# A two-layer decoder kernel: the first attention's bias inside its output product and its weight splits on ScalarE and VectorE, a third buffer for heads, and paired value products in the grouped attentions

## The chip, the cores and the metric

The kernel runs on one core of one Trainium2 chip, as one program. The metric is the device time of one execution in microseconds; the time given for the kernel before is the median of three runs. The engines are TensorE (PE in the rows; PEld is its weight load), VectorE (DVE), ScalarE (ACT), GpSimd (POOL) and SyncE (SP), which issues the DMAs.

## The reference

`x` and a context `ctx` are 16 sequences of 64 tokens with 512 features. Two layers, each an attention, a second attention and a feed-forward part, each added to `x` and followed by a layer norm:

```python
x = ln(x + attn0(x))            # 32 heads of 16, ALiBi bias, causal; qkv and output product have biases
x = ln(x + xattn0(x, ctx))      # 32 query heads, 8 key/value heads of 128, rotary, mask; output product Wo
x = ln(x + ffn0(x))             # dense + 2 of 8 low-rank experts
x = ln(x + attn1(x))            # 32 query heads, 8 key/value heads of 128, causal window of 64
x = ln(x + xattn1(x, ctx))      # one head of 512
x = ln(x + ffn1(x))             # gated, weights of 16 levels, low-rank additions
```

In `attn0` the output is `out @ w_proj + b_proj`. All is in float32; the kernel splits the operands of its large products in a high part (float32r) and a low part (the rest) and adds three products: high by high, high by low, low by high.

## The kernel before, in words

Six stages follow one another: A (`attn0`), B (`xattn0`), C (`ffn0`), D (`attn1`), E (`xattn1`), F (`ffn1`). The change touches A and the function `grouped_attention`, which makes B and D. Each engine has its own queue, written out in program order; semaphores order the engines. Tokens are 1024, in NT = 8 tiles of 128; features are KC = 4 blocks of 128.

Stage A. After the projections there are 32 units n (4 chunks of 8 heads by 8 token tiles). TensorE, for unit n: four transposes of the probabilities (L428), the scores of unit n+3 (`scores`, L376), half a projection of the next chunk's keys or queries (`project`) or, in the last chunk (n from 24), the output product of tile n-24 without its last block (`output_early`) and the last block of the tile before (`output_last`), then the unit's value product (`attend`, L398). VectorE, for unit n: `front(n+2)` (L555 adds the ALiBi bias, L558 maximum, L561 subtract) in turns with `back(n+1)` (L566 sum, L569 reciprocal, L572 scale); in the last chunk also the low parts of the heads (`low_early`, L578 and L579; `low_last`, L583) and the residual (L590). Before unit 0 VectorE adds the output bias `bp` to all eight tiles of `xtok` (L602). ScalarE, for unit n: copy of the transposed probabilities (L521), `move(n-1)` of the heads, exponent of unit n+2 (L484), and in every second unit `keys` (L462, L464 from the bank, then four scaled copies, L469) or `queries` (L477, L479); in the last chunk `split_early` (L503, L504) after the exponent. GpSimd splits the weight blocks in the list `order`, high part (L78) and low part (L317), through two raw buffers which SyncE refills.

Stages B and D. `turn` runs 16 units u for a pair of key/value heads, four turns in all; units 0 to 7 and 8 to 15 are two groups. TensorE, for unit u: transposes (L858), scores of unit u+2 (L825; where u % 4 is 2, `late`, they come after the value product), value product (L870, two matmuls of 64 rows that use halves of the array), output product of unit u-1 (L83 to bankY), a projection of queries (L83 to bankA), and where u % 8 is 7 the unit's own output product at the end. VectorE: in B the rotation (L1013, L1015, L1019), then L1026, L1030, L1033 for the unit after next and L1038, L1041, L1044 for the next, the residual of unit u-2 (L1049), the low part of the heads (L1082), low parts of weights (L1060). ScalarE: copy of the probabilities (L959), in B the swapped halves for the rotation (L910), the heads out of the bank (L967), the exponent of unit u+2 (L922), high parts of weights (L937). `output` waits for the low part of its own heads and for the residual of two units before:

```python
pe.wait_ge(o_low, part.unit(u) + 2)
pe.wait_ge(y_done, part.unit(u) + 1)      # starts at 2
```

Of the kernel before, what the change touches and what calls it, by code (L numbers as in the profile page):

```python
# [15 lines left out]
P = 128  # L16
# [26 lines left out]
def build_program(nc, io):  # L43
# [162 lines left out]
    clamped = sem("A_clamped"); gathered = sem("A_gathered"); small = sem("A_small"); pbias = sem("A_pbias")  # L206
# [6 lines left out]
    with ExitStack() as mem:  # L213
# [9 lines left out]
        oS = [[sb(mem, f"AoS{i}{p}", [P, KC, P], F32R) for p in range(2)] for i in range(2)]  # L223
# [4 lines left out]
        bqk = sb(mem, "Abqk", [P, 2, KC]); bv = sb(mem, "Abv", [P, KC]); bp = sb(mem, "Abp", [P, D])  # L228
        pos = sb(mem, "Apos", [P, NT], I32); row = sb(mem, "Arow", [P, NT], U32)
        own = sb(mem, "Aown", [P, 4])  # L230
        sc = [sb(mem, f"Asc{i}", [P, HEADS, S]) for i in range(3)]
        pt = [sb(mem, f"Apt{i}", [P, D]) for i in range(2)]
# [7 lines left out]
        order += [("qk", i) for i in range(4, 2 * KC)] + [("c", 3)]  # L240
# [22 lines left out]
        with nc.Block() as block:  # L263
            @block.sync
            def _(sp):
# [25 lines left out]
                sp.dma_start(bp[:], io["bp"].to_broadcast([P, D])).then_inc(small, 16)  # L291
# [7 lines left out]
            def _(pool):  # L299
# [3 lines left out]
                for n, x in enumerate(order):  # L303
# [7 lines left out]
                    if kind == "qk" and i >= 2:  # L311
                        pool.wait_ge(a_ready, banks_before(i // 2 - 1, 3 + i % 2))
                    elif kind == "p" and i == 0:
                        pool.wait_ge(a_ready, 4 + NT)
# [18 lines left out]
            def _(pe):  # L333
# [68 lines left out]
                def output_early(t):  # L402
# [7 lines left out]
                    product(bankY[t % 2][:], [x for k in range(KC - 1) for x in three([w[:, k, :] for w in oS[t % 2]], [w[:, k, :] for w in wbig])], stop=False)  # L410

                def output_last(t):
                    pe.wait_ge(o_low, t + 1)
                    product(bankY[t % 2][:], three([w[:, KC - 1, :] for w in oS[t % 2]], [w[:, KC - 1, :] for w in wbig]), start=False).then_inc(y_ready, 1)
# [5 lines left out]
                pe.wait_ge(small, 80)  # L420
# [22 lines left out]
            def _(act):  # L443
# [12 lines left out]
                def keys(c, h):  # L456
# [6 lines left out]
                    for e in range(2):  # L463
                        nc.scalar.activation(kt[HIGH, :, e, :], src[HIGH, :, 1 - e, :], ACT.Identity, bias=bqk[HIGH, 1, c:c + 1]).then_inc(k_moved, 1)  # L464
                    act.wait_ge(k_moved, 3 * (2 * c + h + 1))
# [20 lines left out]
                def move(n):  # L486
# [6 lines left out]
                    else:  # L493
                        if t >= 2:
                            act.wait_ge(y_ready, t - 1)
                        nc.scalar.activation(oS[t % 2][0][:, c, :], src, ACT.Identity, bias=bv[:, c:c + 1]).then_inc(o_high, 1)

                def split_early(t):

                    if t >= 2:  # L500
                        act.wait_ge(y_ready, t - 1)
                    act.wait_ge(o_done, LAST_CHUNK - NT + t + 1)
                    nc.scalar.activation(oS[t % 2][0][:, 0, :], first_o[:, t, :], ACT.Copy).then_inc(e_high, 1)  # L503
                    nc.scalar.activation(oS[t % 2][0][:, 1:KC - 1, :], V[:, 0:KC - 2, t, :], ACT.Copy).then_inc(e_high, 1)  # L504
# [3 lines left out]
                for h in range(2):  # L508
                    keys(0, h)
                    queries(0, h)  # L510
                act.wait_ge(small, 80)
# [5 lines left out]
                for n in range(UNITS):  # L517
# [19 lines left out]
            def _(dve):  # L537
# [12 lines left out]
                def front(n):  # L550
                    s3 = sc[n % 3][:]
                    dve.wait_ge(s_ready, n + 1)
                    if n >= 3:
                        dve.wait_ge(t_ready, n - 2)
# [1171 lines left out]
```

## Time and profile before

| | |
|---|---|
| median of three runs | 1681.94 us (1681.24 to 1682.49) |
| profiled execution | 1676.39 us, span 1674.6 us |
| TensorE busy | 1581.4 us, 94% of the span |
| VectorE busy | 984.5 us, 59% |
| ScalarE busy | 660.6 us, 39% |
| GpSimd busy | 201.2 us, 12% |
| stage A, last matmul of its output product ends | near 200.0 us |
| stage B, first transposes to last output product | 254.23 to 796.63 us |
| stage D, last output product ends | near 1433.9 us |

A share of busy time is an average over stages with different limits. Times in rows are microseconds from the start of the span; busy times overlap for matmuls, whose ends are modelled. A row's number in brackets is how long its engine stood idle before it, and the name behind it what ended that.

### The profile page before, as it was taken

What the parts mean: (1) busy time and instruction counts of PE and PEld (TensorE: products, weight loads), DVE (VectorE), ACT (ScalarE), POOL (GpSimd) and SP (SyncE); (2) the same over time, 40 slices, a digit from 0 to 9 for tenths busy, and PEclk for the clock granted to TensorE, in tenths of its full rate; (3) what the DMA queues carried; (4) which work ended last, traced back from release to release, by engine and by line L of the source; (5) the groups of instructions that cost most, each with busy time, mean ns of one, the idle gap of its engine ahead of it and who ended that gap; (6) DMA issues with size and microseconds to landing.
All of it is one profiled execution on the core that took longest, in us unless ns stands there. A gap on an engine that the chain in (4) does not pass through costs nothing. (4 is left out here: it accounts for less than half of the span.)

```text
span 1674.6 us, 22788 instructions
## 1 busy us (share of the span) xinstructions
PE 1581.4 (94%) x8504; PEld 1267.2 (76%) x8504; DVE 984.5 (59%) x1958; ACT 660.6 (39%) x1209; POOL 201.2 (12%) x146
## 2 busy tenths in 40 slices
PE   8788799999999999999889999999999999889998
PEld 6566587787788778876777788788878877676876
DVE  5998767766765776677433542552453346246755
ACT  4476434433433443333333332332332322436541
POOL 8321040000000000000340000000000000613330
PEclk9899999999999999999999999999999999999999
DMA  6111011101110110100111110110110000202231
GB/s 227 33 33 45 13 51 51 64 14 39 38 51 1 64 51 13 39 13 26 45 52 39 38 51 1 62 50 13 50 50 25 27 25 25 68 20 81 78 85 50
DMA packets 26023, 75.44 MB, mean 45 GB/s; under 512 B 3888, under 2 KB 4624, under 8 KB 25680
## 3 DMA queue, kind: packets, MB, share of 16 engines
q1 hardware_dynamic: 25552, 73.16, 13.2%
q8 instruction: 63, 1.03, 0.3%
q0 software_dynamic: 384, 1.05, 0.2%
q14 instruction: 24, 0.20, 0.0%
HBM read 72.10 MB, written 2.10 MB: 44 GB/s over the span
## 5 line engine op out<-in xcount | busy, mean ns | idle before, releaser
L83 PE MATMUL bankY<-sb_Dwo,sb_DoT 128*128 128x512 f32 x768 | 194.0, 402 | 0.3 <-DVE sb_DoT L1082 0.3
L83 PE MATMUL bankY<-sb_Bwo,sb_BoT 128*128 128x512 f32 x768 | 192.1, 399 | 0.2 <-DVE sb_BoT L1082 0.2
L83 PE MATMUL bankA<-sb_xT,sb_Bwq 128*128 128x512 f32 x768 | 190.5, 397 | 0.5 <-issue 0.5
L83 PE MATMUL bankA<-sb_xT,sb_Dwq 128*128 128x512 f32 x768 | 189.9, 396 | 0.0
L83 PEld LDWEIGHTS bankY<-sb_Dwo,sb_DoT 128*128 128x128 f32 x768 | 141.0, 189 | 42.3 <-issue 13.3
L83 PEld LDWEIGHTS bankY<-sb_Bwo,sb_BoT 128*128 128x128 f32 x768 | 139.9, 188 | 41.6 <-issue 12.9
L83 PEld LDWEIGHTS bankA<-sb_xT,sb_Bwq 128*128 128x128 f32 x768 | 142.3, 188 | 34.8 <-issue 3.6
L83 PEld LDWEIGHTS bankA<-sb_xT,sb_Dwq 128*128 128x128 f32 x768 | 142.2, 188 | 33.9 <-issue 2.7
L1013 DVE TENSOR_TENSOR sb_BqT<-bankA,sb_Btable 128x512 f32<-128x512 f32 x64 | 44.3, 692 | 150.1 <-ACT sb_Bsw L910 150.1
L1049 DVE TENSOR_TENSOR sb_xtok<-sb_xtok,bankY 128x512 f32<-128x512 f32 x128 | 87.2, 681 | 53.0 <-PE bankY L83 52.9
L910 ACT ACTIVATE sb_Bsw<-bankA 64x512 f32<-64x512 f32 x160 | 94.8, 593 | 54.8 <-PE bankA L83 51.7
L1026 DVE TENSOR_TENSOR sb_Dsc<-bankA,sb_Dbound 128x256 f32<-128x256 f32 x64 | 27.0, 421 | 149.0 <-PE bankA L825 149.0
L1082 DVE TENSOR_TENSOR sb_DoT<-bankO,sb_DoT 128x512 fp32r<-128x512 f32 x64 | 43.8, 684 | 117.3 <-ACT sb_DoT L967 117.3
L959 ACT ACTIVATE sb_Dpt<-bankT 128x256 f32<-128x256 f32 x64 | 24.6, 384 | 155.2 <-PE bankT L858 155.2
L825 PE MATMUL bankA<-sb_Bkt,sb_BqT 128*128 128x128 f32 x512 | 69.3, 278 | 8.0 <-DVE sb_BqT L1019 7.8
L78 POOL TENSOR_TENSOR sb_Ew<-sb_raw,sb_zero 128x1024 fp32r<-128x1024 f32 x4 | 7.6, 1894 | 566.1 <-POOLq L730 566.1
L825 PEld LDWEIGHTS bankA<-sb_Bkt,sb_BqT 128*128 128x128 f32 x512 | 62.1, 191 | 14.3 <-DVE sb_BqT L1019 8.7
L922 ACT ACTIVATE sb_Bsc<-sb_Bsc 128x256 f32<-128x256 f32 x64 | 26.7, 417 | 115.5 <-DVE sb_Bsc L1033 115.5
L78 POOL TENSOR_TENSOR sb_Cwar<-sb_raw,sb_zero 128x1024 fp32r<-128x1024 f32 x1 | 1.9, 1894 | 573.9 <-POOLq L730 573.9
L825 PE MATMUL bankA<-sb_Dkt,sb_DqT 128*128 128x128 f32 x512 | 69.0, 278 | 0.0
L825 PEld LDWEIGHTS bankA<-sb_Dkt,sb_DqT 128*128 128x128 f32 x512 | 62.2, 191 | 5.1 <-issue 5.0
L967 ACT ACTIVATE sb_DoT<-bankO 128x512 fp32r<-128x512 f32 x64 | 38.3, 599 | 65.0 <-PE bankO L870 65.0
(277 smaller groups left out, 2969.5 us busy)
## 6 DMA issues: line engine op xcount, KB each, us to landing
sb_raw<-in_w_attn SPq DMA_DIRECT2D x80, 512.0 KB, 3.5
sb_raw<-in_q_gu SPq DMA_DIRECT2D x22, 256.0 KB, 2.7
sb_raw<-in_q_d SPq DMA_DIRECT2D x11, 256.0 KB, 2.6
sb_raw<-in_wqk SPq DMA_DIRECT2D x8, 256.0 KB, 2.6
sb_rawx<-in_xT SPq DMA_DIRECT2D x4, 512.0 KB, 6.4
sb_raw<-in_ctxT SPq DMA_DIRECT2D x4, 512.0 KB, 6.3
sb_xtok<-in_x_tok SPq DMA_DIRECT2D x1, 2048.0 KB, 13.2
sb_raw<-in_ctx_tok SPq DMA_DIRECT2D x4, 512.0 KB, 3.8
```

The source lines that it names most:

```text
L78: return nc.gpsimd.tensor_tensor(dst, src, zero[0:src.shape[0]].to_broadcast([src.shape[0], src.shape[1]]), ALU.add)
L83: last = nc.tensor.matmul(out, lhs, rhs, start=start and i == 0, stop=stop and i == len(pairs) - 1)
L825: done = nc.tensor.matmul(bank[:, at:at + P], qT[:, 2 * t + b, 2 * hp:2 * hp + 2, :].rearrange("p h q -> p (h q)"), window(kt, 2 * t + b, ...
L910: nc.scalar.activation(sw[part.swap(x)][64 * i:64 * i + 64, :], bankA[part.buffer(x)][64 - 64 * i:P - 64 * i, :], ACT.Copy).then_inc(swapp ...
L922: nc.scalar.activation(flat, flat, ACT.Exp, scale=HD ** -0.5).then_inc(st["exp"], 1)
L959: nc.scalar.activation(pt[u % 2][:], bankT[u % 2][:, 0:GROUP * S], ACT.Copy).then_inc(pt_done, 1)
L967: nc.scalar.activation(oT[u % 2][0][:].rearrange("p h b q -> p b h q"), bankO[:, :, 0:GROUP * S].rearrange("p b (h q) -> p b h q", h=GROUP ...
L1013: nc.vector.tensor_tensor(to, bankA[part.buffer(x)][:].rearrange("p (b s) -> p b s", s=S), table[:, 0, half].rearrange("p (b s) -> p b s", ...
L1026: nc.vector.tensor_tensor(s3, bankA[part.buffer(("S", u))][:].rearrange("p (a c) -> p a c", a=2)[:, :, S:S + P], bound_of(u).unsqueeze(1). ...
L1049: nc.vector.tensor_tensor(xtok[:, t, :], xtok[:, t, :], bankY[u % 2][:], ALU.add).then_inc(y_done, 1)
L1082: nc.vector.tensor_tensor(oT[u % 2][1][:].rearrange("p h b q -> p b h q"), bankO[:, :, 0:GROUP * S].rearrange("p b (h q) -> p b h q", h=GR ...
```

## The change

In stage A:
- The output bias is no longer added by VectorE. Two copies of the row `bp` are loaded into the third score buffer, split by ScalarE and VectorE into a high row (0) and a high and low row (32), and each tile's output product begins with a matmul of a block of ones by this block of rows.
- GpSimd splits only the blocks before the projection's; the seven others are split in the loop at fixed units (`IN_LOOP`), the high part on ScalarE (`weights_high`), the low part on VectorE one unit later.
- The heads for the output product have three buffers instead of two, and ScalarE's `split_early` comes before the exponent.
- The scaled copies of the keys come one unit after their move from the bank (`keys_by_head`).

In `grouped_attention`:
- The value products of units u-1 and u are done together in the odd unit, into the two halves of each bank, and one ScalarE and one VectorE instruction empty both. In B the last two units of each group stay alone, in D the last two of all.
- The output product in unit u is that of unit u-2, ahead of the value products; the residual in unit u is that of u-3. ScalarE takes the exponent before it empties the bank.

```diff
-        oS = [[sb(mem, f"AoS{i}{p}", [P, KC, P], F32R) for p in range(2)] for i in range(2)]
+        oS = [[sb(mem, f"AoS{i}{p}", [P, KC, P], F32R) for p in range(2)] for i in range(3)]
+        IN_LOOP = {1: ("p", 0), 4: ("p", 1), 5: ("qk", 4), 8: ("qk", 5), 9: ("c", 3), 13: ("qk", 6), 16: ("qk", 7)}
...
-                for n, x in enumerate(order):
+                for n, x in enumerate(order[:order.index(IN_LOOP[1])]):
...
+                        nc.gpsimd.memset(f32(ones[:]), 1.0).then_inc(pones, 1)
+                        pool.wait_ge(pones, 1)
+                        nc.gpsimd.memset(f32(bp[:]), 0.0).then_inc(pones, 1)
+                        pool.wait_ge(pones, 2)
...
-                    product(bankY[t % 2][:], [x for k in range(KC - 1) for x in three([w[:, k, :] for w in oS[t % 2]], [w[:, k, :] for w in wbig])], stop=False)
+                    if t == 0:
+                        pe.wait_ge(pbias, 3)
+                    product(bankY[t % 2][:], [(ones[:], bp[:])], stop=False)
+                    product(bankY[t % 2][:], [x for k in range(KC - 1) for x in three([w[:, k, :] for w in oS[t % 3]], [w[:, k, :] for w in wbig])], start=False, stop=False)
...
+                def weights_high(x):
+                    kind, i = x
+                    at, _, dst = place(x)
+                    m = through_raw.index(x)
+                    act.wait_ge(w_low, order.index(x))
+                    act.wait_ge(w_raw[m % NRAW], 16 * (m // NRAW + 1))
+                    if kind == "qk":
+                        act.wait_ge(a_ready, banks_before(i // 2 - 1, 3 + i % 2))
+                    elif kind == "p" and i == 0:
+                        act.wait_ge(a_ready, 4 + NT)
+                    nc.scalar.activation(dst[0], at, ACT.Copy).then_inc(w_high, 1)
...
+                for r in (0, 32):
+                    nc.scalar.activation(bp[r:r + 1, :], bpr[r:r + 1, :], ACT.Copy).then_inc(pbias, 1)
...
+                    if n >= LAST_CHUNK - 1 and n - LAST_CHUNK + 1 < NT:
+                        split_early(n - LAST_CHUNK + 1)
                     if n + 2 < UNITS:
                         exp(n + 2)
+                    if n in IN_LOOP:
+                        weights_high(IN_LOOP[n])
                     if n % 2 == 0 and 2 <= n <= LAST_CHUNK:
                         c, i = (n - 2) // NT + 1, (n - 2) % NT // 2
                         (queries if i % 2 else keys)(c, i // 2)
-                    if n >= LAST_CHUNK - 1 and n - LAST_CHUNK + 1 < NT:
-                        split_early(n - LAST_CHUNK + 1)
+                    if n % 4 == 3 and n < LAST_CHUNK:
+                        keys_by_head(n // NT + 1, n % NT // 4)
...
-                for t in range(NT):
-                    nc.vector.tensor_tensor(xtok[:, t, :], xtok[:, t, :], bp[:], ALU.add).then_inc(pbias, 1)
...
+                    if n - 1 in IN_LOOP:
+                        weights_low(IN_LOOP[n - 1])
...
+            def alone(u, final):
+
+                return u % NT >= NT - 2 and (rope or (final and u >= NT))
+
+            def attended(u, last):
+
+                return (u,) if alone(u, last) else (u - 1, u) if u % 2 else ()
...
+                    def attend(part, u):
+
+                        units = attended(u, part.final)
+                        if units and u < NT:
+                            pe.wait_ge(v_done, part.it * 4 + u // 2 + 1)
+                        for v in units:
+                            if v == units[0]:
+                                pe.wait_ge(pt_done, part.unit(u) + 3)
+                                pe.wait_ge(o_low, part.unit(v) + 1)
+                            for b in range(2):
+                                rows = slice(S * b, S * b + S)
+                                done = nc.tensor.matmul(bankO[:, b, side(v)], V[rows, v % NT, v // NT * HD:(v // NT + 1) * HD], pt[v % 2][rows, :], start=True, stop=True)
+                            done.then_inc(o_ready, 1)
...
-                            if u % NT and not late(u):
+                            if u % NT >= 2:
+                                output(part, u - 2)
+                            attend(part, u)
+                            if u % NT == NT - 1 and alone(u, part.final):
                                 output(part, u - 1)
                             for x in banks:
                                 if x[0] != "S" or late(u):
                                     project(part, x)
                             if u % NT == NT - 1:
+                                if not alone(u, part.final):
+                                    output(part, u - 1)
                                 output(part, u)
...
                             if not late(u) and (u + 2 < SLOTS or not part.final):
                                 exp(part, u + 2)
+                            units = attended(u, part.final)
+                            if units:
+                                act.wait_ge(o_ready, part.unit(u) + 1)
+                            if len(units) == 1:
+                                nc.scalar.activation(of_unit(0, u), unit_bank(u), ACT.Copy).then_inc(o_high, 1)
+                            elif units:
+                                nc.scalar.activation(of_pair(0), pair_bank, ACT.Copy).then_inc(o_high, 2)
...
-                            if u % NT >= 2:
-                                residual(part, u - 2)
+                            if u % NT >= 3:
+                                residual(part, u - 3)
...
                             if u % NT == NT - 1:
+                                residual(part, u - 2)
                                 residual(part, u - 1)
```

## Rows read from the trace of the kernel before

**Rows 1.** Busy time by stretch: each engine's us (instructions), granted clock, DMA share, GB/s

```profile
254.23:796.63 542.40, 529.93 (x2776) 424.66 (x2777) 375.23 (x769) 218.49 (x389) 0.00 (x0) 1.00 0.11 36
880.00:1434.00 554.00, 550.72 (x2871) 441.92 (x2870) 250.36 (x565) 177.50 (x327) 0.00 (x0) 1.00 0.10 34
...
1426.70:1433.90 7.20, 7.20 (x26) 5.70 (x25) 2.47 (x6) 4.24 (x7) 0.00 (x0) 0.76 0.01 2
791.05:796.63 5.58, 5.58 (x26) 4.57 (x25) 2.47 (x6) 4.21 (x7) 0.00 (x0) 1.00 0.00 0
61.02:66.25 5.23, 5.23 (x31) 4.04 (x31) 5.23 (x11) 1.49 (x4) 0.00 (x0) 0.59 0.00 0
66.25:69.45 3.20, 3.20 (x36) 2.47 (x30) 2.58 (x5) 2.48 (x6) 0.00 (x0) 1.00 0.04 10
```

**Rows 2.** Timeline of TensorE in stage A: start, us, instructions [idle before]

```profile
61.02 1.12 PE L428 MATMUL bankT<-sb_ident,sb_Asc 128*128 128x128 f32 x4 [10.56 <-DVE sb_Asc L572]
...
78.02 1.10 PE L376 MATMUL bankA<-sb_Akd,sb_Aqz 128*128 128x256 f32 x4 [0.69 <-ACT sb_Aqz L479]
...
150.22 0.66 PE L428 MATMUL bankT<-sb_ident,sb_Asc 128*128 128x128 f32 x4
```

**Rows 3.** Timeline of VectorE in stage A, loop and ahead of it

```profile
41.35 16.50 DVE L602 TENSOR_TENSOR sb_xtok<-sb_xtok,sb_Abp 128x512 f32<-128x512 f32 x8
...
76.30 0.69 DVE L555 SCALAR_TENSOR_TENSOR sb_Asc<-bankA,sb_Aalibi 128x512 f32<-128x512 f32 x1
...
79.41 0.68 DVE L555 SCALAR_TENSOR_TENSOR sb_Asc<-bankA,sb_Aalibi 128x512 f32<-128x512 f32 x1
```

**Rows 4.** Timeline of ScalarE in stage A

```profile
37.92 0.63 ACT L484 ACTIVATE sb_Asc<-sb_Asc 128x512 f32<-128x512 f32 x1 [5.97 <-DVE sb_Asc L561]
...
69.77 2.57 ACT L469 ACTIVATE sb_Akd<-sb_Akt,sb_Aown 128x512 f32<-128x512 f32 x4
```

**Rows 5.** Waits of VectorE from 147 to 199 us: total, times, longest

```profile
DVE sb_AoS L578 <- ACT sb_AoS L504: 10.7, 8, 3.1
```

**Rows 6.** Timeline of VectorE in stage A's last chunk

```profile
164.44 0.69 DVE L555 SCALAR_TENSOR_TENSOR sb_Asc<-bankA,sb_Aalibi 128x512 f32<-128x512 f32 x1
...
170.69 0.69 DVE L555 SCALAR_TENSOR_TENSOR sb_Asc<-bankA,sb_Aalibi 128x512 f32<-128x512 f32 x1
```

**Rows 7.** Groups of instructions by line: busy us, mean ns | idle before

```profile
L572 DVE TENSOR_TENSOR sb_Asc<-sb_Asc,sb_Ari 128x512 f32<-128x512 f32 x32 | 26.2, 820 | 0.0
L561 DVE TENSOR_TENSOR sb_Asc<-sb_Asc,sb_Amx 128x512 f32<-128x512 f32 x32 | 24.3, 759 | 0.0
...
L1060 DVE TENSOR_TENSOR sb_Bwq<-sb_raw,sb_Bwq 128x1024 fp32r<-128x1024 f32 x14 | 17.1, 1220 | 3.5 <-ACT sb_Bwq L937 3.5
...
L937 ACT ACTIVATE sb_Bwq<-sb_raw 128x1024 fp32r<-128x1024 f32 x14 | 14.6, 1044 | 0.0
```

**Rows 8.** Timeline of all engines in stage B, units 0, 1, 2 and 7

```profile
404.11 0.42 DVE L1044 TENSOR_TENSOR sb_Bsc<-sb_Bsc,sb_Bri 128x256 f32<-128x256 f32 x1
...
405.23 0.38 PE L858 MATMUL bankT<-sb_ident,sb_Bsc 128*128 128x128 f32 x2
...
406.44 0.70 PE L870 MATMUL bankO<-sb_Bpt,sb_BV 64*128 64x256 f32 x4
407.07 3.02 PE L83 MATMUL bankY<-sb_Bwo,sb_BoT 128*128 128x512 f32 x12
...
410.67 0.42 ACT L922 ACTIVATE sb_Bsc<-sb_Bsc 128x256 f32<-128x256 f32 x1 [2.78 <-DVE sb_Bsc L1033]
...
417.06 1.16 PE L825 MATMUL bankA<-sb_Bkt,sb_BqT 128*128 128x128 f32 x8 [0.56 <-DVE sb_BqT L1019]
...
451.45 0.38 PE L858 MATMUL bankT<-sb_ident,sb_Bsc 128*128 128x128 f32 x2
...
457.41 0.68 DVE L1049 TENSOR_TENSOR sb_xtok<-sb_xtok,bankY 128x512 f32<-128x512 f32 x1
```

**Rows 9.** Timeline of TensorE at the end of stage D

```profile
1426.07 0.70 PE L870 MATMUL bankO<-sb_Dpt,sb_DV 64*128 64x256 f32 x4 [2.21 <-ACT sb_Dpt L959]
```

More of the change, by code:

```diff
@@ L239, in build_program @@
         order = [("qk", 0), ("qk", 1)] + [("v", k) for k in range(KC)] + [("c", 0), ("c", 1), ("qk", 2), ("qk", 3), ("c", 2), ("p", 0), ("p", 1)]
-        order += [("qk", i) for i in range(4, 2 * KC)] + [("c", 3)]
+        order += [("qk", 4), ("qk", 5), ("c", 3), ("qk", 6), ("qk", 7)]
+        IN_LOOP = {1: ("p", 0), 4: ("p", 1), 5: ("qk", 4), 8: ("qk", 5), 9: ("c", 3), 13: ("qk", 6), 16: ("qk", 7)}
         through_raw = [x for x in order if x[0] != "v"]
@@ L419, in _ @@
                         scores(t - 3)
-                pe.wait_ge(small, 80)
+                pe.wait_ge(small, 96)
                 for n in range(UNITS):
@@ L509, in _ @@
                     keys(0, h)
+                    keys_by_head(0, h)
                     queries(0, h)
-                act.wait_ge(small, 80)
+                act.wait_ge(small, 96)
+                act.wait_ge(pones, 2)
+                for r in (0, 32):
+                    nc.scalar.activation(bp[r:r + 1, :], bpr[r:r + 1, :], ACT.Copy).then_inc(pbias, 1)
                 exp(0)
@@ L599, in _, with weights_low @@
                 in_turns(front(1), back(0))
+                dve.wait_ge(pbias, 2)
+                nc.vector.tensor_tensor(bp[32:33, :], bpr[32:33, :], f32(bp[32:33, :]), ALU.subtract).then_inc(pbias, 1)
                 dve.wait_ge(in_tok, 16)
-                for t in range(NT):
-                    nc.vector.tensor_tensor(xtok[:, t, :], xtok[:, t, :], bp[:], ALU.add).then_inc(pbias, 1)
+                def weights_low(x):
+                    at, _, dst = place(x)
+                    dve.wait_ge(w_high, order.index(x) + 1)
+                    nc.vector.tensor_tensor(dst[1], at, f32(dst[0]), ALU.subtract).then_inc(w_low, 1)
                 for n in range(UNITS):
@@ L704, in grouped_attention @@
             pt = [sb(mem, f"{tag}pt{i}", [P, GROUP * S]) for i in range(2)]
-            oT = [[sb(mem, f"{tag}oT{i}{p}", [P, GROUP, 2, S], F32R) for p in range(2)] for i in range(2)]
+            oT = [sb(mem, f"{tag}oT{p}", [P, 2, GROUP, 2, S], F32R) for p in range(2)]
             mx = sb(mem, f"{tag}mx", [P, 2, 4]); sm = sb(mem, f"{tag}sm", [P, 2, 4]); ri = sb(mem, f"{tag}ri", [P, 2, 4])
@@ L834, in output @@
                         pe.wait_ge(y_done, part.unit(u) + 1)
-                        pairs = [x for h in range(GROUP) for x in three([o[:, h].rearrange("p b q -> p (b q)") for o in oT[u % 2]], [w[:, h, :] for w in wo])]
+                        pairs = [x for h in range(GROUP) for x in three([o[:, u % 2, h].rearrange("p b q -> p (b q)") for o in oT], [w[:, h, :] for w in wo])]
                         if u % NT == NT - 1:
@@ L861, in turn @@
                                 project(part, banks[0])
-                            if late(u):
-                                output(part, u - 1)
-                            if u < NT and u % 2 == 0:
-                                pe.wait_ge(v_done, part.it * 4 + u // 2 + 1)
-                            pe.wait_ge(pt_done, part.unit(u) + 3)
-                            pe.wait_ge(o_low, part.unit(u) + 1)
-                            for b in range(2):
-                                rows = slice(S * b, S * b + S)
-                                done = nc.tensor.matmul(bankO[:, b, 0:GROUP * S], V[rows, u % NT, u // NT * HD:(u // NT + 1) * HD], pt[u % 2][rows, :], start=True, stop=True)
-                            done.then_inc(o_ready, 1)
-                            if u % NT and not late(u):
+                            if u % NT >= 2:
+                                output(part, u - 2)
+                            attend(part, u)
+                            if u % NT == NT - 1 and alone(u, part.final):
                                 output(part, u - 1)
@@ L976, in turn @@
                                 queries_or_keys(part, x)
-                            if part.final and u == SLOTS - 2:
-                                ln_roots(act, norm + 1, 0)
                             if part.final and u == SLOTS - 1:
```

64 lines of the change are left out of this document (38 added, 26 removed).

## The prediction

> **What bounds the kernel now.** I read the busy time by stretch first. TensorE is busy 530 of 542 us in the first grouped attention (stage B) and 551 of 554 in the second (stage D) [rows 1]: there a change pays only if TensorE's queue gets shorter or waits less. The first attention (stage A) is different. TensorE's timeline shows an idle gap of 10.56 us ahead of unit 1's transposes, released by VectorE [rows 2], and VectorE's timeline shows what stood ahead of that release: eight additions of the projection's bias, 16.50 us in one run [rows 3]. After that the loop is a close race: a unit costs TensorE 3.20 us when nothing waits [rows 1] and VectorE 3.11 us (76.30 to 79.41) [rows 3]. ScalarE is the third runner: its four copies of keys take 2.57 us in one run [rows 4], and its late queries stall the scores by 0.69 us [rows 2]. The last chunk (units 24 to 31) is VectorE's: its first operation of a unit starts at 164.44 and again at 170.69, a period of 6.25 us [rows 6], and it waits there for ScalarE's split of the earlier heads, 10.7 us over eight units [rows 5].
>
> **Part 1, the bias.** The additions go: 16.5 us of VectorE, of which TensorE feels its 10.56 us gap; the slow unit behind it (5.23 us at a mean granted clock of 0.59, so partly at the lower level of 1.2 GHz, instead of 3.20 at 1.00 [rows 1]) gives 2.0 more. In their place come eight matmuls of 512 columns, 0.23 us each (24 of them take 5.58 [rows 1]), in units where TensorE waits for VectorE. The two one-row copies on ScalarE come before its first exponent, where it idles 5.97 us [rows 4]; uncovered they would cost 1.3. VectorE's one-row subtraction costs at most one 0.69 us operation. GpSimd's two memsets stand behind a larger one and delay its next splits by under 1 us; those are not used before 48 us.
>
> **Part 2, the splits of weights.** GpSimd's seven splits inside the loop go to ScalarE (1.04 us for a 1024-wide block) and VectorE (1.22) [rows 7]; 512-wide ones I take as half and a bit, 0.6 each. Three wide and four narrow: 6 us on VectorE, 5.5 on ScalarE. Against it VectorE gets back what it loses beside GpSimd: its loop's two operations with both inputs in SBUF have means of 0.82 and 0.76 us over 32 [rows 7] where the period of 3.11 has room for 0.69 each, so 4.2 + 2.2 = 6.4 us. The row agrees with the Trainium skill (page SBUF — State Buffer, section Who interferes with whom): a VectorE instruction with two SBUF inputs contends with a GpSimd one that reads SBUF. By that rule the excess goes wholly, and the sum would be the same.
> ScalarE's order gets worse at one place. In unit 4 it now has the key copies left from unit 3, the exponent, the split of block p1 and only then the queries: exponent done 2.7 us into the unit, plus 1.0, plus 1.6 for the queries is 5.3, where the scores of unit 8 want them at 3.7, and they were 0.7 late before. Walked through the queues that gives stalls of some 2.3 us in the first chunk and 1.2 to 1.5 in each later half-chunk; the 0.7 us lag of the copy behind the keys goes. Four units then take 14.1 to 14.5 us (15.8 the first time), where four without any wait are 12.8. Unit 1 starts where the gap begins now, at 50.4, so unit 24 starts at 50.4 + 3.2 + 15.8 + 14.05 + 14.3 + 14.45 + 14.1 + 6.4 = 132.7 us; today it starts at 150.22 [rows 2]. Gain so far 17.5 us, the 10.56 and 2.0 of part 1 in it.
>
> **Part 3, the third buffer.** The early split moves ahead of the exponent and needs the output product of three tiles before, not two. Both are there in time, so VectorE's wait of 0.6 us in a middle unit goes: 6.25 becomes 5.6, still above TensorE's some 5.0. Six such units give 3.9 us, the longer waits of the first two and the last (the rest of the 10.7) 4 more, and unit 24's late queries take back 1. Gain 7. Stage A in all: -24 us. Bounds: -15 (queries twice as late in every chunk) and -30 (all of VectorE's ledger, 16.5 + 10.7 + 6.4 less 6 above, felt, with its clock).
>
> **Part 4, stage B.** Here I count a loss. Today unit 1 of a group of eight runs transposes, scores, its value product, the output product of unit 0, queries. Afterwards unit 0 has no value product, unit 1 has both, and the output product of unit 0 comes first in unit 2. What it needs is late. ScalarE takes the exponent of unit 3 before it empties the pair's bank, and that exponent waits for VectorE's subtraction behind the rotary chain: it starts at 410.67, 5.44 us into unit 1 (405.23) [rows 8]. Emptying 1024 columns takes then 1.05 us and VectorE's low part 1.22 [rows 7]: the output product can start 8.1 us into unit 1. TensorE's own work before it is 1.21 (405.23 to 406.44) + 2 x 0.63 (406.44 to 407.07) + 2.8 for twelve matmuls: 5.3; bank and probabilities, which come out of the same chain, hold it until 5.8, and it then stands for 2.2 us. ScalarE's split of the next weights (1.04) delays unit 2's copy and swaps as well; the rotary chain takes as long as today, so the scores of unit 4 come 11.7 us into unit 1, against 11.83 now (405.23 to 417.06) [rows 8]. Equal time, but an output product (2.85) and a value product (0.63) are still to be done; unit 0 was 0.63 shorter, which VectorE's probabilities (404.11 + 0.42) just allow. Loss 3.48 - 0.15 - 0.63 = 2.7 us, 3.0 in second groups, where unit 0 gains less: 23 us for eight groups.
> The second wait is in the last unit of a group. The output product of unit 6 needs the residual of unit 4, which moved on VectorE from unit 6 to unit 7 (from u-2 to u-3), behind that unit's rotary chain: the residual there starts at 457.41, 5.96 us into the unit (451.45), and takes 0.68 [rows 8]. TensorE is there after 1.2 + 2.85 + 0.63 = 4.7. Stall 2.0 us, seven times (the last group has no rotation there): 14 us. Behind both waits stand the next projections in TensorE's queue, so nothing covers them.
>
> **Part 5, what a pair saves.** A pair issues the same eight instructions as two units. The bounds are nothing and what entering and leaving the half-array costs: 0.63 less two passes, each near one 512-wide matmul (0.23), is 0.17 us. I take it for 31 pairs in D and 16 in B (the other eight end in the wait above): 8 us, rounded down to -5 and -2. By the Trainium skill (TensorEngine Tiling (Array Packing), Key Properties) a change of tiling mode drains the array; then every pair saves its 0.17, which no run so far shows. What ScalarE and VectorE save is off the path.
>
> **Part 6, stage D.** The same order without a rotary chain: the exponent is early, the output product of unit 0 0.15 us late, eight times: +1. The residual of unit 4 is done long before. In the final group the pairs' emptying is not covered by queries (1.2 and 2.2 us), while the 2.21 us wait for pt [rows 9] is: +1. With part 5: -3.
>
> **Part 7, the clock.** Behind that 2.21 us wait 24 matmuls take 7.20 us at a mean clock of 0.76; the same 24 in B take 5.58 at 1.00 [rows 1]: 1.6 us. B gets 15 waits of nearly that length. Bounds 0 and +24; I take two, +3.
>
> **Sum.** -24 + 23 + 14 - 2 - 3 + 3 = +11 us. The profiled execution is 1676.39 us around a span of 1674.6; the median of the runs is 1681.94, 5.55 higher. So the span goes to 1685 and the median to 1692, rounded down. 0.2% is 3.4 us, about what a measurement of this kernel can tell from no change.
>
> **Rivals.** (a) The first wait of B is not there: if ScalarE could empty the pair while it waits for the exponent's input, 23 us of loss go and the time is 1669. For it speaks D, where the same order has room; against it ScalarE's queue, in which the exponent stands ahead. It decides once B costs under 23 us in all. (b) The first attention gives 15, its low end, as the queries are late in every chunk: 1701. (c) The lower clock follows most of B's waits: 15 more, 1707. (d) Pairs save their 0.17 everywhere and A gives 29: 1683, no change that can be told.
>
> **How the numbers follow.** Forecast with its own range of 1685 to 1700: 0.5; (a) 0.2, (b) 0.1, (c) 0.07, (d) 0.13. Faster is (a), 0.2; same (d) and a shade of the forecast, 0.14; slower the rest, 0.66. The range leaves out the far half of (a) and the end of (c): 1673 to 1707.
>
> **What would show it.** Stage A ends near 176 us instead of 200, without VectorE's long run at 41 us, and TensorE's idle there names the queries. In B TensorE has a new wait of the output product for sb_BoT's low part, eight times near 2 us, and one for sb_xtok, seven times near 2 us; B is some 34 us longer, D some 3 shorter. The prediction is wrong if the first output product of a group follows the queries at once, or if stage A ends above 185.

## The result and the profile after

The kernel after takes 1690.29 us (median of five runs, 1688.24 to 1694.5) against 1681.94 (five runs, 1680.12 to 1683.02): the ratio is 1.0053, with a 95% interval of 1.0036 to 1.0069. So it is slower by 8.4 us; 1692 was forecast.

The traced execution of after is a long one of its kind, 1694.5 us with a span of 1692.7, while that of before was a short one. The two traces are 18.1 us apart, the medians 8.4: after's trace is 4.2 us above its median and before's 5.6 below. What follows splits up the 18.1 us of the traces; no trace shows where the other 9.7 lie.

The same stretches of after by windows, as in [rows 1]: first attention up to its last chunk, last chunk, stage B from its first transposes to its last output product, stage D from its first transposes to its last output product, and two output products of the same 12 matmuls:

```profile
51.13:133.38 82.25, 76.72 (x697) 58.15 (x691) 79.27 (x147) 66.44 (x132) 0.00 (x0) 0.98 0.11 33
133.38:178.09 44.71, 37.74 (x290) 28.01 (x285) 36.40 (x83) 20.65 (x49) 7.83 (x8) 1.00 0.08 24
232.30:820.89 588.59, 541.50 (x2777) 433.38 (x2778) 377.28 (x743) 209.50 (x363) 0.00 (x0) 0.97 0.10 33
925.23:1449.88 524.65, 519.70 (x2777) 424.49 (x2777) 247.06 (x523) 164.23 (x285) 0.00 (x0) 1.00 0.11 36
404.25:408.66 4.41, 4.41 (x12) 3.48 (x13) 3.76 (x7) 1.00 (x2) 0.00 (x0) 0.61 0.33 119
784.56:787.38 2.82, 2.82 (x12) 2.33 (x13) 2.68 (x6) 0.07 (x1) 0.00 (x0) 1.00 0.00 0
```

Stage D between the same two points in the kernel before:

```profile
899.66:1433.90 534.24, 530.96 (x2777) 425.69 (x2777) 247.22 (x556) 171.69 (x317) 0.00 (x0) 1.00 0.11 36
```

TensorE's timeline in stage A, to be read beside [rows 2]:

```profile
51.13 0.66 PE L436 MATMUL bankT<-sb_ident,sb_Asc 128*128 128x128 f32 x4
...
67.20 2.04 PE L381 MATMUL bankA<-sb_Akd,sb_Aqz 128*128 128x256 f32 x4 [2.13 <-ACT sb_Aqz L490]
...
82.77 1.10 PE L381 MATMUL bankA<-sb_Akd,sb_Aqz 128*128 128x256 f32 x4 [0.92 <-ACT sb_Aqz L490]
...
133.38 0.65 PE L436 MATMUL bankT<-sb_ident,sb_Asc 128*128 128x128 f32 x4
...
178.09 1.04 PE L168 MATMUL bankT<-sb_ident,sb_xtok 128*128 128x128 f32 x8
```

Stage A ends at 178.09 instead of 199.98, a gain of 21.9 us. Stage B took 542.40 us [rows 1] and takes 588.59, 46.2 more. Between the ends of B and D 637.3 us became 629.0 (1433.90 less 796.63; 1449.88 less 820.89), 8.3 less: D itself is 9.6 shorter (534.24 less 524.65) and stage C, between them, 1.3 longer (104.34 for 103.03). The rest, behind D, is 2.1 longer. Together: -21.9 + 46.2 - 8.3 + 2.1 = 18.1.

Stage B's loss has two parts. TensorE's idle time there went from 12.5 us (542.40 less 529.93) to 47.1 (588.59 less 541.50), 34.6 more, and its busy time grew by 11.6. TensorE's waits in B, total, times, longest:

```profile
PE bankY L83 <- issue: 15.7, 8, 2.0
PE bankY L83 <- DVE sb_xtok L1121: 15.0, 7, 2.1
```

Both stand ahead of output products. The first names no releaser, so the queues have to be read. All engines at units 1 and 2 of B's second turn:

```profile
396.06 0.38 PE L931 MATMUL bankT<-sb_ident,sb_Bsc 128*128 128x128 f32 x2
...
401.49 0.42 ACT L990 ACTIVATE sb_Bsc<-sb_Bsc 128x256 f32<-128x256 f32 x1 [3.40 <-DVE sb_Bsc L1105]
401.81 1.01 ACT L1042 ACTIVATE sb_BoT<-bankO 128x1024 fp32r<-128x1024 f32 x1
401.85 0.20 PEld L931 LDWEIGHTS bankT<-sb_ident,sb_Bsc 128*128 128x128 f32 x2 [0.36 <-DVE sb_Bsc L1116]
...
402.92 1.23 DVE L1159 TENSOR_TENSOR sb_BoT<-bankO,sb_BoT 128x1024 fp32r<-128x1024 f32 x1 [1.13 <-ACT sb_BoT L1042]
...
404.25 4.58 PE L83 MATMUL bankY<-sb_Bwo,sb_BoT 128*128 128x512 f32 x12 [1.96 <-issue]
```

The exponent starts 5.43 us into unit 1 (396.06), ScalarE empties the pair's bank behind it, VectorE's low part ends at 404.15, and the output product of unit 0 follows 0.10 us later, 8.19 us into unit 1. That is the chain of the prediction (5.44 and 8.1). And the product then takes 4.41 us at a mean granted clock of 0.61, so for the most part at the level of 1.2 GHz, where a later one with the same wait takes 2.82 at 1.00.

### The profile page after: what moved, and what is told of

The parts are those of the page before. It is cut to its first block and busy times, and to the rows that moved or that the text cites. A ratio compares the mean times of both kernels' runs of the same rounds, so it can differ in the third digit from the quotient of the medians.

```text
span 1692.7 us, 22741 instructions
## 1 busy us (share of the span) xinstructions
PE 1583.0 (94%) x8512; PEld 1277.1 (75%) x8512; DVE 971.0 (57%) x1903; ACT 651.3 (38%) x1163; POOL 178.9 (11%) x134
## 5 line engine op out<-in xcount | busy, mean ns | idle before, releaser
L83 PE MATMUL bankY<-sb_Bwo,sb_BoT 128*128 128x512 f32 x768 | 205.3, 420 | 34.1 <-issue 15.7
L83 PEld LDWEIGHTS bankY<-sb_Bwo,sb_BoT 128*128 128x128 f32 x768 | 149.6, 201 | 70.2 <-issue 35.3
L83 PE MATMUL bankY<-sb_Dwo,sb_DoT 128*128 128x512 f32 x768 | 190.5, 399 | 4.2 <-DVE sb_DoT L1159 3.4
L1159 DVE TENSOR_TENSOR sb_DoT<-bankO,sb_DoT 128x1024 fp32r<-128x1024 f32 x31 | 38.0, 1225 | 65.3 <-ACT sb_DoT L1042 65.3
L83 PE MATMUL bankY<-sb_xT,sb_Awqk 128*128 128x512 f32 x168 | 51.8, 445 | 8.0 <-DVE sb_xT L572 7.4
```

The source lines that it names most:

```text
L83: last = nc.tensor.matmul(out, lhs, rhs, start=start and i == 0, stop=stop and i == len(pairs) - 1)
L1159: nc.vector.tensor_tensor(of_pair(1), pair_bank, f32(of_pair(0)), ALU.subtract).then_inc(o_low, 2)
```

## The experiments

Each kernel is given by its difference from the one named. Times are medians; the kernel before ran beside every group of kernels, at 1680.9 to 1682.0 us. Ratios are to it.

**The stages apart.** `a_alone` has the new first attention and the old `grouped_attention`, whole functions put together; `grouped_alone` the other way round. `b_old_d_paired` is the kernel after with this in `grouped_attention`, so that B goes in its old order:

```diff
-                return u % NT >= NT - 2 and (rope or (final and u >= NT))
+                return rope or (u % NT >= NT - 2 and final and u >= NT)
...
-                            if u % NT >= 2:
+                            if rope and late(u):
+                                output(part, u - 1)
+                            if not rope and u % NT >= 2:
                                 output(part, u - 2)
                             attend(part, u)
-                            if u % NT == NT - 1 and alone(u, part.final):
+                            if (u % NT and not late(u)) if rope else (u % NT == NT - 1 and alone(u, part.final)):
                                 output(part, u - 1)
...
-                            if u % NT >= 3:
-                                residual(part, u - 3)
+                            if u % NT >= (2 if rope else 3):
+                                residual(part, u - (2 if rope else 3))
```

and with the exponent behind the emptying where `rope`. `b_old_d_single` differs from it in `alone`, which returns True everywhere.

`a_alone`:

> All of the change in the first attention, with the grouped attentions as they were. Theory (the stages add up as the two traces show): stage A ends 21.9 us earlier, its last output product near 178 us, nothing else moves, so the time is 1682 - 22 = 1660 us. Rival (A's gain is partly given back where B starts, because its weights and tables are loaded and split no earlier than before): B's first transposes would start later than 232 and the time would be 1668 or more. By my prediction's step it would be 1658.

`grouped_alone`:

> All of the change in the grouped attentions, with the first attention as it was. Theory (16 new waits in B near 2 us each, 35 us, plus a lower clock behind about half of them, 12 us; pairs save 8 us in D): 1682 + 46 - 8 = 1720 us. Rival (the lower clock behind B's waits belongs to the one execution that was traced, not to the waits): +35 - 8, 1709 us, and the products behind the waits take 3.0 us instead of 4.5.

`b_old_d_paired`:

> The kernel after with the order of before in B alone: there every unit has its own value product, output product one unit later, ScalarE empties the bank before the exponent, residual of u-2. A and D are as in the kernel after. Theory (all of the loss is B's order): B from its first transposes to its last output product is 542 us again, no wait of its output products over 1 us; 1690 - 46 = 1644 to 1652 us by the median. Rival (half of the loss is the pairs themselves or the load of B by the faster A): 1665 or more.

`b_old_d_single`:

> As the kernel with B in its old order and D paired, but D's value products are done one unit at a time too, at their new place behind the output product of u-2. It tells what in D saves its 1.4 us for eight units. Theory (the pair saves it, entering and leaving the half-array less often, 0.35 us for each of 31 pairs and no less): 9 us slower than with pairs. Rival (the new order saves most, because the output product now comes ahead of the value product and its operands are always there; a pair only saves 0.20, 1.26 less 1.06): 3 to 6 us slower. If the order saves all, the same time.

Measured: `a_alone` 1660.29 us, ratio 0.9869 (0.9854 to 0.9885). `grouped_alone` 1711.97, 1.0184 (1.0170 to 1.0198). `b_old_d_paired` 1651.06, 0.9823 (0.9810 to 0.9837). `b_old_d_single` 1654.58, 0.9842 (0.9829 to 0.9856).

The two halves of the change, against the 1680.94 beside them, are -20.7 and +31.0, together +10.4, where the whole change measured +8.4. As ratios they give 0.9869 + 1.0184 - 1 = 1.0053, that of the whole change: the stages add up, and no loss shows where they meet. The first theory for `grouped_alone` (1720) was 8 us too high and its rival (1709) 3 too low. The new waits are all there (8 of 15.7 us in all, 7 of 15.0), but only 5 of the 16 waits near 2 us were followed by a slow product in its trace, where after had 10. The number differs from one execution to the next; that it isn't zero is common to both. With B in its old order the loss is gone: B takes 546.2 us up to its last output product (542.4 before; the gaps told of at the end are in it) and the kernel is 39 us faster than after.

In D the four-way comparison separates order and pair. Two units of D without pairs and with them (start, us, instructions):

```profile
1110.93 0.38 PE L931 MATMUL bankT<-sb_ident,sb_Dsc 128*128 128x128 f32 x2
1111.15 1.06 PE L884 MATMUL bankA<-sb_Dkt,sb_DqT 128*128 128x128 f32 x8
1111.96 2.98 PE L83 MATMUL bankY<-sb_Dwo,sb_DoT 128*128 128x512 f32 x12
1114.87 0.70 PE L912 MATMUL bankO<-sb_Dpt,sb_DV 64*128 64x256 f32 x4
1115.50 3.12 PE L83 MATMUL bankA<-sb_Dwv,sb_xT 128*128 128x256 f32 x24
```

```profile
1106.64 3.00 PE L83 MATMUL bankY<-sb_Dwo,sb_DoT 128*128 128x512 f32 x12
1109.47 3.05 PE L83 MATMUL bankA<-sb_Dwv,sb_xT 128*128 128x256 f32 x24
...
1119.11 1.13 PE L912 MATMUL bankO<-sb_Dpt,sb_DV 64*128 64x256 f32 x8
1120.17 3.06 PE L83 MATMUL bankA<-sb_xT,sb_Dwq 128*128 128x512 f32 x12
```

From start to start, a value product alone holds TensorE 0.63 us (1114.87 to 1115.50) and a pair 1.06: 0.20 less than two. And the output product ahead of a value product takes 2.91 us, one ahead of a projection 2.83, so not entering the half-array in the even unit saves 0.08 more: 0.28. Over a group of eight units, from first transposes to first transposes, D's later first groups take 59.94 us before, 59.84 in the new order one by one and 58.56 with pairs: 1.28 for four pairs, 0.32 each. The last eight units are another matter. From their first transposes to the last output product they take 45.84 us before, with the wait and the slowed products of [rows 9], 41.16 one by one, where TensorE never waits (busy 41.16 of 41.16 us), and 45.91 with pairs. From the first to the last transposes of these units alone it is 31.82 us one by one and 36.56 with pairs; before (35.35) can't be set beside these two, as one output product more lies in its stretch. Over D the pairs win 4.2 us on the new order alone (529.01 to 524.78), which in turn wins 5.2 on before (534.24), 4.7 of them in the last eight units. By the median pairs gain 3.5. The theory of 9 us was wrong in its total and its rival of 3 to 6 right, but the other way round for a single pair: it saves 0.32 us, near the theory's 0.35 and not the rival's 0.20. Half of what pairs earn in D they give back in its last eight units.

**The parts of stage A.** Three kernels undo one part each of `a_alone`: the bias (`xtok` gets it from VectorE again, the `ones` matmul goes), the splits, the third buffer (with ScalarE's early split behind the exponent again, which the last cut below leaves out).

```diff
-        IN_LOOP = {1: ("p", 0), 4: ("p", 1), 5: ("qk", 4), 8: ("qk", 5), 9: ("c", 3), 13: ("qk", 6), 16: ("qk", 7)}
+        IN_LOOP = {}
...
-                for n, x in enumerate(order[:order.index(IN_LOOP[1])]):
+                for n, x in enumerate(order):
```

```diff
-        oS = [[sb(mem, f"AoS{i}{p}", [P, KC, P], F32R) for p in range(2)] for i in range(3)]
+        oS = [[sb(mem, f"AoS{i}{p}", [P, KC, P], F32R) for p in range(2)] for i in range(2)]
```

`a_bias_undone`:

> The first attention of the change alone (the kernel a_alone, 1660.3 us), but with the output bias added by VectorE to all eight tiles ahead of the loop, as before. Theory: the 16.5 us run of additions is back and TensorE waits some 10 us ahead of unit 1, with one slow unit behind it (+12.5); the eight matmuls of 0.23 us go, hidden in part: 1672 us. Rival (what is saved there only makes later units wait, since VectorE is the runner in the loop anyway): under 6 us lost. It also takes the eight matmuls out of TensorE's program: if the gaps of 2.0 us without a releaser that a_alone has at the start of B's second and third turn, and the kernel before has not, hang on where the loop's code lies, they move or go.

`a_splits_undone`:

> The first attention of the change alone, but all weight blocks split by GpSimd again. Theory: VectorE's two operations beside GpSimd grow to 0.8 us again, but ScalarE's queries come earlier; unit 24 starts 4 us later: 1664 us. Rival (VectorE's and ScalarE's own splits cost as much as GpSimd's contention): within 2 us of 1660. TensorE's program has the same instructions as in a_alone, so the gaps at the start of B's turns stay as they are.

`a_third_undone`:

> The first attention of the change alone, but with two buffers for the heads and ScalarE's early split behind the exponent. Theory: the last chunk's unit takes 6.25 us again instead of 5.55, stage A ends 5 to 7 us later, 1667 us. Rival (the other parts gave VectorE the room already): within 2 us of 1660, the period stays near 5.6.

Measured: 1660.55, 1661.52 and 1662.37 us, ratios 0.9875 (0.9860 to 0.9890), 0.9882 (0.9867 to 0.9898) and 0.9882 (0.9866 to 0.9897): not to be told from `a_alone`. The theories for the bias (1672) and the buffer (1667) are out, and that for the splits (1664) is not met. In the traces each costs 3 us at the end of stage A: the layer norm's first transposes start at 176.69 in `a_alone`, at 179.69, 179.91 and 179.73 in the three. These costs are good to some 1 us only: the last chunk of `a_alone` holds a stretch at the lower clock (45.83 us at a mean of 0.96) and takes 44.6 to 44.7 in the seven other kernels with the same stage A; against those the third buffer is worth 3.9 us there (48.54 without it, at 1.00). So the three make 9 to 11 of the 23.3 us which `a_alone` gains. The rest isn't a sum of parts, and the additions of the bias say why. First the tile of the bias in the kernel before, then in `a_bias_undone` (duration in ns, least, median, most), and TensorE's wait there:

```profile
L602 DVE TENSOR_TENSOR sb_xtok<-sb_xtok,sb_Abp x8: 678/2381/2890, 41.3 to 55.0; 128x512 f32<-128x512 f32 x8
```

```profile
L621 DVE TENSOR_TENSOR sb_xtok<-sb_xtok,sb_Abp x8: 677/678/680, 46.0 to 50.2; 128x512 f32<-128x512 f32 x8
```

```profile
54.08 0.66 PE L427 MATMUL bankT<-sb_ident,sb_Asc 128*128 128x128 f32 x4 [2.34 <-DVE sb_Asc L591]
```

The same eight additions take 4.89 us in one run instead of 16.50 [rows 3]. In the kernel before GpSimd splits weights up to 57.3 us, and an addition beside it takes 2.4 us; with the splits in the loop GpSimd has done at 45.5, before the additions start. So either edit takes most of the gap at unit 1 away, and undoing the bias alone costs 3.9 us there (54.1 for 50.2), undoing the splits alone 0.2 (50.4). The rule of the Trainium skill that the prediction used for the loop's operations (page SBUF — State Buffer, section Who interferes with whom) names this form as well, an operation of VectorE with both inputs in SBUF beside GpSimd; here the trace agrees, at 2.38 us for 0.678. And it agrees for the loop's two operations: over the 23 units from 51 to 133 us of after they have means of 0.692 and 0.684 us for 0.76 and 0.82 [rows 7], so the excess is gone whole.

```profile
L594 DVE TENSOR_TENSOR sb_Asc<-sb_Asc,sb_Amx 128x512 f32<-128x512 f32 x23 | 15.9, 692 | 0.0
L605 DVE TENSOR_TENSOR sb_Asc<-sb_Asc,sb_Ari 128x512 f32<-128x512 f32 x23 | 15.7, 684 | 0.0
```

`a_third_undone` has its period back: VectorE waits for ScalarE's split in six units, 4.7 us in all, and TensorE's units take 6.25 us, 161.0 to 167.3, instead of 5.55.

**The two waits of B.** `residual_first` and `empty_first` are the kernel after with one edit each, for B only; `both_first` has both:

```diff
+                            early = rope and u % NT == NT - 1
+                            if early:
+                                residual(part, u - 3)
                             in_turns(rotate(part, *banks) if rope and banks else None,
...
-                            if u % NT >= 3:
+                            if u % NT >= 3 and not early:
                                 residual(part, u - 3)
```

```diff
-                            if not late(u) and (u + 2 < SLOTS or not part.final):
-                                exp(part, u + 2)
                             units = attended(u, part.final)
+                            first_empty = rope and len(units) == 2
+                            if not first_empty and not late(u) and (u + 2 < SLOTS or not part.final):
+                                exp(part, u + 2)
...
+                            if first_empty and not late(u) and (u + 2 < SLOTS or not part.final):
+                                exp(part, u + 2)
```

`residual_first`:

> The kernel after (1690.3 us), with the residual of unit 4 ahead of the rotary chain in the last unit of each of B's groups. Theory (TensorE's seven waits of 2.1 us for that residual go, and the lower clock behind five of them with 1.5 us each): 15 + 7 less, 1668 us, and no wait of B's output products names the residual. Rival (the residual, now ahead of the chain, delays the next probabilities by its own 0.68 us and the wait moves there): 1680 or more. Rival for the clock (as many products are slowed, elsewhere): 1675.

`empty_first`:

> The kernel after, with ScalarE emptying a pair of B ahead of the exponent. Theory (ScalarE is then free 1.1 us earlier for the pair, VectorE's low part starts when its chain ends, 1.13 us sooner): eight waits of 1.96 become 0.8, 9 us, and if the lower clock doesn't follow a wait that short, up to 7 more for five slowed products: 1674 to 1681 us. Rival (the exponent of unit 3, behind the emptying, is then what the next probabilities wait for): within 3 us of 1690.

`both_first`:

> The kernel after, with both edits. Theory: the sum of both, 1655 to 1660 us, and the granted clock in B is 1.00. Rival (the stretches at the lower clock come at a rate of their own, whatever the waits): 1667 or more.

Measured: 1670.82 us, ratio 0.9947 (0.9934 to 0.9959); 1680.77, 0.9997 (0.9989 to 1.0006); 1660.63, 0.9881 (0.9867 to 0.9895). Against after that is 19.5, 9.5 and 29.7 us less: the two edits add up. The first lies between its theory (1668) and the rival for the clock (1675), the second at the upper end of its theory (1674 to 1681), the third 0.6 us above the 1655 to 1660 of its own. TensorE's waits in B in `both_first`:

```profile
PE bankY L83 <- issue: 5.9, 8, 0.7
```

The seven waits for the residual are gone, and the eight for the pair fell from 1.96 to 0.74. In B's stretch at large (first transposes to last output product) after took 588.6 us, `residual_first` 563.5, `empty_first` 575.5, `both_first` 554.9; 12.5 us more than before remain. Of the 25.1 us of the first edit 14.3 are idle time and 10.8 busy time, of which the theory had 7.

These runs also show what the clock follows. Of the waits of 1.96 us or more ahead of an output product, a slow one came behind 10 of 16 in after, 5 of 16 in `grouped_alone`, 3 of 9 in `residual_first`, 4 of 8 in `empty_first`; behind the waits of 0.74 us none, of 8 and 8. In `both_first` the only slowed product of B follows its only wait of over 2 us, in the last group. So the rival in which slow stretches come at a rate of their own is out.

**Versions meant to be faster.** In `d_last_single` D's last eight units go one by one; `queries_first` is that kernel with ScalarE's weight split behind the queries.

```diff
-                return rope or (u % NT >= NT - 2 and final and u >= NT)
+                return rope or (final and u >= NT)
```

```diff
-                    if n in IN_LOOP:
-                        weights_high(IN_LOOP[n])
                     if n % 2 == 0 and 2 <= n <= LAST_CHUNK:
                         c, i = (n - 2) // NT + 1, (n - 2) % NT // 2
                         (queries if i % 2 else keys)(c, i // 2)
+                    if n in IN_LOOP:
+                        weights_high(IN_LOOP[n])
```

`d_last_single`:

> The kernel b_old_d_paired (1651.1 us), with the value products of D's last eight units done one by one in the new order. In the traces the last eight units took 36.56 us with pairs, 31.82 one by one, 35.31 in the kernel before. Theory (the pairs' late emptying is uncovered there, as no queries are projected): 4.7 us faster, 1646 us. Rival (the pairs of the group before shift that wait to its start): under 2 us.

`queries_first`:

> The kernel d_last_single (1643.3 us), with ScalarE's high part of the next weight block behind the queries in units 4, 8 and 16 of the first attention, where both fall in one unit. Theory (the split of 1.04 or 0.57 us ahead of the queries is what makes them later than in the kernel before): TensorE's waits for the queries in the first three chunks, 2.1 and four of about 0.9, together 5.2 us, become 1.1 and four of 0.3 to 0.9, under 3.5 us in all, the slow unit behind the 2.1 us wait may go as well (2 us), and unit 24 starts 2 to 4 us earlier; 1640 us. Rival (keys and queries are as late as the exponent ahead of them): the waits stay at 5 us and the time within 1 us of 1643.

Measured: 1643.25 us, ratio 0.9773 (0.9760 to 0.9786), and 1642.57, ratio 0.9779 (0.9765 to 0.9793). The first is 7.8 us under `b_old_d_paired`, of which its last eight units, 31.85 instead of 36.56 us, explain 4.7 as forecast. The other 3 aren't placed: the two traces are 5.5 us apart, and outside D they differ by 1.2 more ahead of it and 2.0 less behind it, in stages that the edit doesn't touch. TensorE in unit 4 of stage A in `queries_first`, to be read beside the row of 67.20 above:

```profile
65.02 1.10 PE L381 MATMUL bankA<-sb_Akd,sb_Aqz 128*128 128x256 f32 x4 [1.18 <-ACT sb_Aqz L490]
```

That wait shrank from 2.13 us to 1.18, as the theory had it, but the five together only from 5.2 to 4.3, not under 3.5. Counted from unit 1, unit 24 starts 2.1 us earlier (80.0 for 82.1), but 1.4 of them are the lower clock behind the 2.13 us wait: in `a_alone`, where the clock stayed at 1.00 behind that wait, it is 80.7. The times of the kernels don't tell the two apart. Both beat the kernel before and the kernel after.

## Why the prediction was right

The mechanisms forecast were there, and so were most of the prices. That 1692 came within 2 us of 1690.29 is in part luck, as the sum at the end of this section shows.

**Stage A as a whole.** Forecast -24, measured -21.9 in after's trace and -23.3 in `a_alone`'s. Unit 1 started at 51.13 (50.4 forecast), unit 24 at 133.38 (132.7), the last chunk's units took 5.55 us (5.6), the stage ended at 178.1 (176). The queries' waits came where they were put: 2.13 in the first chunk for 2.3, then 0.86 to 0.92 for 1.2 to 1.5; four units with one took 14.0 us, the low end of 14.1 to 14.5, and the first four 17.2 for 15.8, as a lower clock followed the 2.13 us wait (15.6 in `a_alone`, where it didn't). From unit 24 on the gain was 5.1 us, not 7.

**How it was shared out in A was wrong.** The step that failed is that of part 1, by which the bias is worth its 10.56 us gap and 2.0 more. Undoing it costs 3.9 us at unit 1, since 11.6 of the 16.5 us were GpSimd's contention, which part 2 removes too. I read 16.50 us for eight additions and never divided it by eight: 2.06 us for an operation of a size that takes 0.69 elsewhere in the same rows. For the same reason VectorE's one-row subtraction, put at 0.69 us at most, took 2.26 beside GpSimd. Part 3 held in its period and is worth 3.0 to 3.9 us by itself rather than 7. The total came out because the trace was walked from unit to unit.

**The first wait of B.** Forecast eight times 2.2 us, measured eight times 1.96, at the place and by the chain given. Rival (a) is out.

**The second.** Forecast seven times 2.0 us behind the residual, measured seven times 2.14, and moving that one residual took it away.

**The clock.** This term was mis-sized. I took two slow products, +3, with bounds of 0 and 24. There were ten in after's trace (busy time in B 11.6 more) and five in `grouped_alone`. Rival (c) has the lower clock behind most of B's waits. That was so in the one traced execution, but its time of 1707 was not reached in any of the five (1694.5 at most), as D and the medians took back what the clock cost.

**What a pair saves.** Also mis-sized: 0.17 forecast, 0.32 measured, because the pair itself is 0.20 shorter and the even unit enters no half-array. D gained 9.6 instead of 3. Its seven groups ahead of the last gained 9.7, of them 0.1 each through the order. The last eight units lost nothing (45.89 for 45.84; +1 forecast), with TensorE waiting 1.25 and 2.15 us for the pairs' emptying (1.2 and 2.2 forecast); what I didn't see is that one by one they gain 4.7. Here the rule of mode changes that the prediction cited (the Trainium skill, TensorEngine Tiling (Array Packing), Key Properties) goes the same way as the rows: each pair does save time.

**Sum.** In the traces: A -21.9 (forecast -24), waits of B and what hangs on them +34.6 (+37 less 2), clock +11.6 (+3), C and D -8.3 (-3), the rest +2.1 (0): 18.1 instead of 11. The misses on clock and D cancel in part, and the medians, at 8.4, are nearer to each other than the traces by 9.7 us which no trace explains. So the terms bear the sign and the rough size out, and the last few us of the agreement are luck. Rival (d) adds up to some 1685 by its own terms, not 1683; neither time was met, and A gave 21.9, not 29.

## What to carry to other kernels

Where TensorE is busy 98% of a stage, pairing work to save 0.3 us a pair is worth less than one 2 us wait for eight units: list what each moved product now waits for, and find the order in which the engine that feeds it empties its queue. Divide a long run of equal operations by their number first; if one is three times its usual length, as here beside GpSimd, look for an engine at work beside it, since two edits may then claim the same gain. Use an order only in the stages and the groups where its feeding chain has room; here that version is 2.3% faster than before.

## What the runs showed that was not expected

**Gaps at the start of a loop's turn.** B's second and third turn, the second and third pass of its loop, have a gap that names no releaser some 1.2 us into the pass. In `a_alone`:

```profile
377.51 1.01 PE L864 MATMUL bankA<-sb_Bkt,sb_BqT 128*128 128x128 f32 x7
380.50 0.38 PE L864 MATMUL bankA<-sb_Bkt,sb_BqT 128*128 128x128 f32 x1 [1.98 <-issue]
```

It splits one score product in two after seven of its eight matmuls, and in that trace a slow projection of 4.60 us came behind it. The eleven kernels with the bias in the output product, after among them, have gaps of 1.16 to 1.98 us there, which differ between kernels whose TensorE program is the same. The kernel before has 0.18 and 0.36, `a_bias_undone`, without those eight matmuls, 0.69 and 0.18, and `grouped_alone` none. D, with the same loop, has none anywhere. So the long gaps go with the eight matmuls that stand ahead of the loop in TensorE's program, as far as these fourteen kernels show. The Trainium skill (Runtime: NRT & Kernel Launch, Instruction fetch mechanics) has a taken branch stall on the fetch of its target when that lies outside what is loaded. That may be behind the gaps, but no run shows it: they come nine matmuls into the pass and not at its first, and why some kernels have none was not tested. With the lower clock that followed both of them in `a_alone` they eat 2 to 7 us of what stage A gains, and they are most of why undoing the bias costs nothing in the kernel's time (B takes 546.1 us there and 550.9 in `a_alone`).

**The clock falls behind some 2 us waits and not behind others.** Waits of 1.96 us or more were followed by a lower clock, 1.5 us each, in 23 of 50 cases, counted over the traces of the five kernels with paired products in B; waits of 0.74 in none of 16. What decides it is open. Nor is it shown to be what spreads after's executions over 6 us: only one was traced, and the mean granted clocks of the five (0.979 to 0.981) don't follow their times; the lowest belongs to the second shortest, 1688.76 us.
